# Gates between two layers: normalisation moved to ACT in blocks, products without a reader on PE, and an early table load

## The reference

```python
mask = top-20 channels of the context, per batch and position   # 0 or 1, (B, 32, 512)
crucial, rest = mask * xn, (1 - mask) * xn                      # xn = layernorm(x)
def gate(f, factor):
    z = conv1d(concat([max over channels of f, mean over channels of f * factor]), w)   # 7 taps, one output channel
    mu = mean(z); var = mean((z - mu) ** 2)                     # over all 64 * 512 values
    return sigmoid(relu((z - mu) * rsqrt(var + eps) * gamma + beta))
x = x + crucial * gate(crucial, 32 / 20) + rest * gate(rest, 32 / 12)
x = x + attention(layernorm(x)); x = x + layernorm(x) @ (W * block_mask).T
```

## Time and profile before

| | |
|---|---|
| median of three runs | 2092.75 us (2090.44 to 2094.00) |
| the profiled execution, its own time | 2093.99 us |
| its span | 2092.2 us |
| granted TensorE clock, mean | 0.987 of full |
| busy | PE 96%, DVE 62%, ACT 35%, POOL 33% |
| the gates' block, from layer 0's last reduction to layer 1's first DVE work | 1817.8 to 1835.4 us |

### The profile page before, as it was taken

How to read it: one execution, slowest core, us unless ns; L and a number is a source line. 1 busy time by engine, 2 the same in 40 slices (tenths; PEclk the granted TensorE clock), 3 DMA queues, 4 the chain that set the end, 5 groups by cost and what they waited for, 6 DMA issues and landing times. The chain is left out here.

```text
span 2092.2 us, 36562 instructions
## 1 busy us (share of the span) xinstructions
PE 2013.9 (96%) x11300; PEld 1564.8 (75%) x11300; DVE 1295.4 (62%) x4403; ACT 741.6 (35%) x2037; POOL 683.3 (33%) x1068
## 2 busy tenths in 40 slices
PE   7999999999999999999999999999899999779998
PEld 5878788887877888788787878887566666455664
DVE  3846548474564847547484664847477777667774
ACT  2434334343443434334343433433232323122232
POOL 4422324232332423323242332423332333133332
PEclk9999999999999999999999999999999999889999
DMA  7101001010010101001010010111100000000000
GB/s 295 32 15 34 22 24 30 24 30 24 24 30 14 40 14 31 23 24 30 24 30 24 24 30 14 31 46 41 46 1 1 1 0 30 1 1 21 21 15 26
DMA packets 51995, 62.19 MB, mean 30 GB/s; under 512 B 14193, under 2 KB 47665, under 8 KB 51042
## 3 DMA queue, kind: packets, MB, share of 16 engines
q1 hardware_dynamic: 51938, 61.46, 9.3%
HBM read 54.00 MB, written 4.29 MB: 28 GB/s over the span
## 5 line engine op out<-in xcount | busy, mean ns | idle before, releaser
L431 PE MATMUL psLane<-hid,WkT 128*128 128x289 f32 x1536 | 402.4, 407 | 0.0
L431 PEld LDWEIGHTS psLane<-hid,WkT 128*128 128x128 f32 x1536 | 283.3, 190 | 72.3
L644 ACT ACTIVATE probs<-psLane,nmax 128x289 f32<-128x289 f32 x256 | 126.2, 498 | 429.7 <-DVE nmax L751 429.7
L610 ACT ACTIVATE KT<-psLane 96x289 f32<-96x289 f32 (+2 forms) x384 | 155.8, 406 | 151.0 <-PE psLane L431 148.8
L353 POOL TENSOR_TENSOR w_o<-w_o 128x192 f32<-128x192 f32 x64 | 44.8, 700 | 460.6 <-ACT w_o L619 460.6
L789 DVE MAX8 top<-work 128x8 f32<-128x257 f32 x512 | 180.2, 414 | 2.7
L314 POOL TENSOR_TENSOR tails<-probs,unit 128x66 f32<-128x66 f32 x128 | 38.2, 299 | 431.0 <-ACT probs L644 400.2
L421 PE MATMUL psLane<-xnT,WqT 128*128 128x128 f32 x1536 | 176.6, 275 | 0.0
L421 PEld LDWEIGHTS psLane<-xnT,WqT 128*128 128x128 f32 x1536 | 174.7, 192 | 0.3 <-issue 0.3
L518 PE MATMUL psLane<-WoT,OT 128*128 128x512 f32 x384 | 169.2, 597 | 1.4 <-DVE OT L769 1.4
L774 DVE TENSOR_TENSOR X<-X,psLane 128x512 f32 (+1 forms) x16 | 11.0, 687 | 254.2 <-PE psLane L518 254.2
(11 more groups left out here) (211 smaller groups left out, 4129.6 us busy)
## 6 DMA issues: line engine op xcount, KB each, us to landing
hid<-in_ctxT SPq DMA_DIRECT2D x64, 514.0 KB, 3.8
y<-X SPq DMA_DIRECT2D x16, 256.0 KB, 2.0
X<-in_x SPq DMA_DIRECT2D x1, 3840.0 KB, 14.1
WqT<-in_WqT SPq DMA_DIRECT2D x4, 768.0 KB, 11.2
WoT<-in_WoT SPq DMA_DIRECT2D x1, 3072.0 KB, 20.9
Vtail<-Vlat SPq DMA_DIRECT2D x128, 24.0 KB
w_qkv<-in_w_qkv SPq DMA_DIRECT2D x2, 1536.0 KB, 6.3
w_ffn<-in_w_ffn SPq DMA_DIRECT2D x2, 1024.0 KB, 6.9
```

The source lines that it names most:

```text
L431: mm = pe.matmul(out[:, 0:S], WkT[:, c, P * k:P * k + P], hid[:, j, c, :], start=(c == 0), stop=(c == DC - 1))
L610: ins = act.activation(KT[at:at + hi - lo, j % 2, g, :], psKV[lo:hi, kv_bank(t, 7 * j + k), 0:S], ACT.Copy)
L644: act.activation(probs[:, g, :], psS[:, g % 2, 0:S], ACT.Exp, bias=nmax[:, g:g + 1], scale=XSCALE, accum_out=rsum[:, j % 2, g:g + 1]).then ...
```

## The change

`ones` is filled with -1/(B*D) instead of 1.0, so that a product with it gives minus a mean. A new helper `keep_busy` issues n products of `ones` with itself into a part of PSUM that nobody reads; 50 of them are added: 10 at the end of layer 0, 6 after the first sum, 12 after the second, and in layer 1, for tile 0 alone, 8 ahead of `turn_mix`, 10 ahead of `turn1` and 4 ahead of `qkv`. Each stands ahead of the wait of its stage.

In `mix_gates` the convolution's four column blocks lie in four banks with a semaphore step each. DVE multiplies a quarter of `w_ffn` by its mask, waits for a block and reduces it straight from PSUM; PE adds the four partial sums in one accumulated group. The squares are made by two activations from PSUM with minus the mean as bias and an accumulator. The power is one instruction of two columns. DVE makes a scale and an offset of two columns, and ACT applies relu with both from PSUM and then sigmoid, for the rest's part first, straight into `blend`, then for the crucial part; DVE is left with one subtraction. An activation of one column with Sigmoid stands at the head of the block, and one with Exp at the head of layer 1 on ACT.

```diff
@@ -899,7 +899,7 @@
         mix_gates(nc, neghalf, ps, Y, ones, blend, early["band"], affine, late, late_in)
-        layer1(nc, a, X, mask, ident, neghalf, x_tile, ps, bufs, blend, late)
+        layer1(nc, a, X, mask, ident, neghalf, x_tile, ps, bufs, blend, late, ones)
@@ -1077,7 +1077,7 @@
                 pool.wait_ge(zero_done, 5)
-                pool.memset(ones[:], 1.0).then_inc(ones_done, 1)
+                pool.memset(ones[:], -1.0 / (B * D)).then_inc(ones_done, 1)
                 pool.wait_ge(ones_done, 1 + 2 * TB)
@@ -1189,6 +1189,8 @@
                 "lora_up": lora_up, "turn3": lambda t, u: norm_turn(pe, n3, t, u, xn, high(u), ident)})
+            pe.wait_ge(ones_done, 1 + 2 * TB)
+            keep_busy(pe, ps[:, LANES - 1], ones, 10)
...
+def keep_busy(pe, out, ones, n):
+
+    for _ in range(n):
+        pe.matmul(out[:, 0:P], ones[:], ones[:], start=True, stop=True)
...
@@ -1360,88 +1368,95 @@
-        part = sb("part", [P, 2])
+        part = sb("part", [P, DC, 2])
+        squares = sb("squares", [P, 2])
+        minus_mean = sb("minus_mean", [P, 2])
-        step, mean_step = sem("mix_step"), sem("mean_step")
-        conv_done, sums_done, pow_done = sem("conv_done"), sem("sums_done"), sem("mix_pow_done")
-        sig_done = sem("sig_done")
-        conv = ps[:, 0, 0:DC * 2 * B]
-        sums = ps[:, 1, 0:2]
-        sums2 = ps[:, 2, 0:2]
...
+        conv = ps[:, 0:DC, 0:2 * B]
+        by_which = conv.rearrange("p c (w b) -> p w c b", w=2)
+        sums = ps[:, 0, 512:514]
+        sums2 = ps[:, 1, 512:514]
+        idle = ps[:, LANES - 1, 512:1024]
...
         def _(pe):
-            pe.wait_ge(mean_step, 2)
+            pe.wait_ge(means_done, 2)
             for o in range(DC):
                 pairs = [(i, ch) for i in (o - 1, o, o + 1) if 0 <= i < DC for ch in range(2)]
                 for n, (i, ch) in enumerate(pairs):
                     at = P * (o - i + 1)
-                    mm = pe.matmul(conv[:, 2 * B * o:2 * B * (o + 1)], band[:, ch, at:at + P],
+                    mm = pe.matmul(conv[:, o], band[:, ch, at:at + P],
                                    Y[:, i, ch].rearrange("p w b -> p (w b)"), start=(n == 0), stop=(n == len(pairs) - 1))
-            mm.then_inc(conv_done, 1)
-            pe.wait_ge(step, 2)
-            pe.matmul(sums, ones[:], part[:], start=True, stop=True).then_inc(sums_done, 1)
-            pe.wait_ge(step, 6)
-            pe.matmul(sums2, ones[:], part[:], start=True, stop=True).then_inc(sums_done, 1)
+                mm.then_inc(conv_done, 1)
+            pe.wait_ge(part_done, DC)
+            for o in range(DC):
+                mm = pe.matmul(sums, ones[:], part[:, o], start=(o == 0), stop=(o == DC - 1))
+            mm.then_inc(sums_done, 1)
+            keep_busy(pe, idle, ones, 6)
+            pe.wait_ge(squares_done, 2)
+            pe.matmul(sums2, ones[:], squares[:], start=True, stop=True).then_inc(sums_done, 1)
+            keep_busy(pe, idle, ones, 12)
 
         @block.gpsimd
         def _(pool):
-            pool.wait_ge(step, 7)
-            for w in range(2):
-                ins = pool.tensor_tensor(rstd[:, w:w + 1], moment[:, w:w + 1], neghalf[:], ALU.pow)
-            ins.then_inc(pow_done, 1)
+            pool.wait_ge(moment_ready, 1)
+            pool.tensor_tensor(rstd[:], moment[:], neghalf[:].to_broadcast([P, 2]), ALU.pow).then_inc(pow_done, 1)
 
         @block.scalar
         def _(act):
-            act.wait_ge(step, 9)
-            act.activation(Z[:].rearrange("p c w b -> p (c w b)"), Z[:].rearrange("p c w b -> p (c w b)"),
-                           ACT.Sigmoid).then_inc(sig_done, 1)
+            act.activation(scratch[:, 0:1], neghalf[:], ACT.Sigmoid).then_inc(scratch_done, 1)
+            act.wait_ge(mean_ready, 1)
+            for w in range(2):
+                act.activation(sq[:, :, w], by_which[:, w], ACT.Square, bias=minus_mean[:, w:w + 1],
+                               accum_out=squares[:, w:w + 1]).then_inc(squares_done, 1)
+            act.wait_ge(scale_done, 1)
+            act.wait_ge(offset_step, 2)
+            for k, w in enumerate((1, 0)):
+                act.activation(Z[:, :, w], by_which[:, w], ACT.Relu, bias=offset[:, w:w + 1], scale=scale[:, w:w + 1])\
+                    .then_inc(relu_done, 1)
+                act.wait_ge(relu_done, k + 1)
+                act.activation(blend[:, :, 0] if w else Z[:, :, 0], Z[:, :, w], ACT.Sigmoid).then_inc(sig_done, 1)
...
         @block.vector
         def _(dve):
...
             dve.wait_ge(late_in, 16 * LATE_LOADS)
-            dve.tensor_tensor(late["w_ffn"][:], late["w_ffn"][:], late["ffn_mask"][:], ALU.mult)
-            dve.wait_ge(conv_done, 1)
-            z = Z[:].rearrange("p c w b -> p (c w b)")
-            dve.tensor_copy(z, conv).then_inc(step, 1)
-            dve.wait_ge(step, 1)
-            dve.tensor_reduce(part[:], Z[:].rearrange(by_which), AX.XY, ALU.add).then_inc(step, 1)
+            for o in range(DC):
+                dve.tensor_tensor(late["w_ffn"][:, o], late["w_ffn"][:, o], late["ffn_mask"][:, o], ALU.mult)
+                dve.wait_ge(conv_done, o + 1)
+                dve.tensor_reduce(part[:, o], conv[:, o].rearrange("p (w b) -> p w b", w=2),
+                                  AX.X, ALU.add).then_inc(part_done, 1)
             dve.wait_ge(sums_done, 1)
-            dve.tensor_scalar(moment[:], sums, 1.0 / count, None, ALU.mult).then_inc(step, 1)
-            dve.wait_ge(step, 3)
-            dve.tensor_tensor(Z[:].rearrange("p c w b -> p c w b"), Z[:],
-                              moment[:].unsqueeze(1).unsqueeze(3).to_broadcast([P, DC, 2, B]), ALU.subtract)\
-                .then_inc(step, 1)
-            dve.wait_ge(step, 4)
-            dve.tensor_tensor(sq[:], Z[:], Z[:], ALU.mult).then_inc(step, 1)
-            dve.wait_ge(step, 5)
-            dve.tensor_reduce(part[:], sq[:].rearrange(by_which), AX.XY, ALU.add).then_inc(step, 1)
+            dve.tensor_scalar(minus_mean[:], sums, 1.0, None, ALU.mult).then_inc(mean_ready, 1)
             dve.wait_ge(sums_done, 2)
-            dve.tensor_scalar(moment[:], sums2, 1.0 / count, EPS, ALU.mult, ALU.add).then_inc(step, 1)
+            dve.tensor_scalar(moment[:], sums2, -1.0, EPS, ALU.mult, ALU.add).then_inc(moment_ready, 1)
             dve.wait_ge(pow_done, 1)
-            dve.tensor_tensor(Z[:], Z[:], rstd[:].unsqueeze(1).unsqueeze(3).to_broadcast([P, DC, 2, B]), ALU.mult)\
-                .then_inc(mean_step, 1)
-            dve.wait_ge(mean_step, 3)
-            dve.tensor_scalar(z, z, affine[:, 0:1], affine[:, 1:2], ALU.mult, ALU.add).then_inc(step, 1)
-            dve.wait_ge(step, 8)
-            dve.tensor_scalar(z, z, 0.0, None, ALU.max).then_inc(step, 1)
-            dve.wait_ge(sig_done, 1)
-            dve.tensor_copy(blend[:, :, 0, :], Z[:, :, 1, :])
-            dve.tensor_tensor(blend[:, :, 1, :], Z[:, :, 0, :], Z[:, :, 1, :], ALU.subtract)
+            dve.tensor_scalar(scale[:], rstd[:], affine[:, 0:1], None, ALU.mult).then_inc(scale_done, 1)
+            dve.wait_ge(scale_done, 1)
+            dve.tensor_tensor(offset[:], minus_mean[:], scale[:], ALU.mult).then_inc(offset_step, 1)
+            dve.wait_ge(offset_step, 1)
+            dve.tensor_scalar(offset[:], offset[:], affine[:, 1:2], None, ALU.add).then_inc(offset_step, 1)
+            dve.wait_ge(sig_done, 2)
+            dve.tensor_tensor(blend[:, :, 1, :], Z[:, :, 0, :], blend[:, :, 0, :], ALU.subtract)
...
+def layer1(nc, a, X, mask, ident, neghalf, x_tile, ps, bufs, blend, late, ones):
...
+        scratch = sb("scratch1", [P, 1])
...
+            def busy_until_first(t, n):
+
+                if isinstance(t, int) and t == 0:
+                    keep_busy(pe, high(LANES - 1), ones, n)
+
             def turn_mix(t, u):
+                busy_until_first(t, 8)
                 pe.wait_ge(s["mixed"], t + 1)
...
+            def turn1(t, u):
+                busy_until_first(t, 10)
+                norm_turn(pe, n4, t, u, xn, high(u), ident)
+
             def qkv(t, u):
+                busy_until_first(t, 4)
                 pe.wait_ge(n4["xnT"], t + 1)
...
             over_lanes(pe, SLOTS1, STARTS1, {
-                "turn_mix": turn_mix, "turn1": lambda t, u: norm_turn(pe, n4, t, u, xn, high(u), ident), "qkv": qkv,
+                "turn_mix": turn_mix, "turn1": turn1, "qkv": qkv,
...
+            act.activation(scratch[:], neghalf[:], ACT.Exp).then_inc(s["table_loaded"], 1)
             over_lanes(act, SLOTS1, STARTS1, {"xnT1": evac_xnT(n4), "evac_qk": evac_qk, "exps": exps, "spread_p": spread_p,
```

More of the change, by code:

```diff
@@ L1362, in mix_gates @@
         sq = sb("sq", [P, DC, 2, B])
-        part = sb("part", [P, 2])
+        part = sb("part", [P, DC, 2])
+        squares = sb("squares", [P, 2])
+        minus_mean = sb("minus_mean", [P, 2])
         moment = sb("moment", [P, 2])
         rstd = sb("mix_rstd", [P, 2])
-        step, mean_step = sem("mix_step"), sem("mean_step")
```

(45 more changed lines are left out.)

## The result

The changed kernel takes 2087.10 us (median of 8 runs, 2085.75 to 2089.41), the kernel before 2093.54 us beside it (8 runs, 2090.44 to 2095.88). The ratio is 0.9970, with a 95% interval of 0.9961 to 0.9979: 6.3 us faster, between 4.4 and 8.2. The profiled execution took 2086.80 us (span 2085.0, clock 0.995), against 2093.99.

A forecast was written before the change was run, and what follows sets the result against it. PE is busy 96% of the span; a serial chain of 17.6 us between the layers leaves it idle or slow. Gates 4.6 plus opening 1.8, less 1.7 for one slow-clock stay, is 4.7 off 2092.75: 2088.05 us, range 2085.3 to 2091.5.

The forecast's parts named there:

- rival A: The clock stays up everywhere behind 1818: 6.4 us won, 2086.3 us; chance 0.27.
- The gates' sum: Gates' block between the layers, PE at 1.00: layer 1 starts at 1830.8 instead of 1835.41, 4.6 us won.
- Moving it to ACT wins nothing: Gates' part behind the power, moved to ACT: lasts 3.4 us, as before.
- The opening's sum: Layer 1's opening at 1.00: Q, K and V begin at 8.75 as before and are 1.8 us shorter.
- The feared stay near 1835 to 1839: Around layer 1's start: one dip of the clock expected there, otherwise 1.00 for most of 1823 to 1850.
- idle products on the chain of waits: Sign that the forecast is wrong; the sum itself had 0.5 us lost to the ten before the first normalised tile.
- the table: Exponential table load of 1.28 us, moved to layer 1's head: already hidden, worth 0 (bounds 0 to 0.3).
- the tail's ten products: Layer 0's tail: they run under DVE's reductions, 1813.3 to 1817.8 at 0.50, 0.1 us at most past DVE.
- I take one: One stay at clock 0.50 on PE's path, costing 1.7 us, so 6.4 - 1.7 = 4.7 us won.
- C: Transposes do not hold the clock in layer 1's opening: 2.1 us won, 2090.65 us; chance 0.14.
- E: Clock at 0.50 from convolution to Q and K, twelve products outlast ACT: 9.3 us lost, 2102.0 us; chance 0.04.
- D: Idle products get in the way or ACT's chain is dearer: 2.9 to 3.8 us won, about 2089.5; chance 0.13.

The follow-up runs named there:

- e14: The changed kernel, unaltered, run again beside others: 2088.05 us, ratio 0.9964 to the kernel before.
- e12: The kernel before, unaltered, run once for a second profile: 2095.55 us profiled, no ratio.
- e6: The changed kernel without the early exponential activation at layer 1's head, run once: 2088.18 us profiled, no ratio.
- e1: The changed kernel without any of the 50 idle products and without the early exponential table: 2090.02 us, ratio 0.9984 to the kernel before.
- e10: The changed kernel with 12 more products at the head of layer 0's PE stream: 2086.31 us, ratio 0.9966 to the kernel before.
- e11: The change with 12 products at layer 0's head, 16 ahead of its last transposes, 6 instead of 10 ahead of `turn1`: 2087.33 us, ratio 0.9963 to before.
- e4: The changed kernel with each idle product turned into a transpose of the same size: 2090.64 us, ratio 0.9990 to the kernel before.
- e2: The kernel before with the 50 idle products put into the old gates and same places: 2090.53 us, ratio 0.9986 to the kernel before.
- e7: The changed kernel with 16 more products ahead of layer 0's last `turn3`: 2087.81 us, ratio 0.9976 to the kernel before.
- e13: The change with scale, offset and maximum on DVE and only the sigmoids on ACT, run once: 2087.95 us profiled, no ratio.
- e3: The changed kernel without the 8, 10 and 4 products at layer 1's opening: 2088.15 us, ratio 0.9970 to the kernel before.
- e5: The changed kernel without the 10 products at layer 0's tail: 2090.63 us, ratio 0.9989 to the kernel before.

## Why the prediction was right, and where it was off

It gave 2088.05 us in 2085.3 to 2091.5, and 4.7 us won; 2087.10 and 6.3 were measured, inside the range. Its 4.7 lies in the measured 4.4 to 8.2, near the lower end. The best estimate is the size of rival A (6.4), but not A's mechanism. That the total came out inside the range is in part luck: up to tile 1's Q and K the change's two profiles win 4.6 and 6.2 us (a and b, against the first profile of before), and c, which the sum held at nothing, wins 3.0 and 1.3 more.

**The gates' sum held.** The timeline of e14, where the convolution ran at 1.00, shows the case that was summed:

```profile
1821.38 4.73 PE L1398 MATMUL psLane<-Y,band 128*128 128x128 f32 x40 [1.24 <-DVE Y L1435]
...
1826.15 0.29 DVE L1441 TENSOR_REDUCE part<-psLane 128x2 f32<-128x128 f32 x1
...
1827.78 0.47 ACT L1420 ACTIVATE sq<-psLane,minus_mean 128x256 f32<-128x256 f32 x1 [5.50 <-DVE minus_mean L1444]
...
1828.60 0.20 ACT L1420 ACTIVATION_READ_ACCUMULATOR sq<-psLane,minus_mean 128x1 f32 x1
...
1829.51 0.70 POOL L1413 TENSOR_TENSOR mix_rstd<-moment,neghalf 128x2 f32<-128x2 f32 x1 [10.32 <-DVE moment L1446]
...
1830.70 0.23 DVE L1452 TENSOR_SCALAR mix_offset<-mix_offset,affine 128x2 f32<-128x2 f32 x1
1831.03 0.56 ACT L1425 ACTIVATE Z<-psLane,mix_offset,mix_scale 128x256 f32<-128x256 f32 x1 [2.23 <-DVE mix_offset L1452]
...
1833.70 0.69 DVE L1640 TENSOR_TENSOR lanes<-mask,blend 128x512 f32<-128x512 uint8 x1 [0.30 <-PEq L1362]
```

| step | predicted, us | e14, us |
|---|---|---|
| convolution's start to the last reduction's end | 5.06 | 5.06 |
| four sums and minus the mean | 1.35 | 1.34 |
| two squares | 1.05 | 1.02 |
| second sum and moment | 0.65 | 0.71 |
| power, two columns | 0.60 | 0.74 |
| three tiny DVE steps | 0.65 | 0.78 |
| relu, sigmoid, twice | 2.05 | 1.92 |
| subtraction and exit | 0.70 | 0.75 |
| convolution's start to layer 1 | 12.11 | 12.32 |

The power was sized from a one-column row of 0.55; with two columns it is 0.70. "Moving it to ACT wins nothing" held too: 3.49 us from the power's end to layer 1, against 3.39 in e12.

**The opening's sum held**: 1.8 predicted, 17.26 - 15.43 = 1.83 measured, and 15.43 (to 0.01) in all six other profiles that have the new gates and layer 1's products as the change has them. The eight products are free (they end at 1835.09, `turn_mix` starts at 1835.27). The ten hold `turn1` back: it starts 7.61 us after layer 1's start instead of 6.97, 0.64 where 0.5 was predicted, and the faster transposes give most of it back. The feared stay near 1835 to 1839 came in no profile of the change. One of the forecast's own signs of being wrong, idle products on the chain of waits, did come, at the price that the sum had given them.

**Terms taken as free that held**: the table (e6), the extra table loads (one load of 1.28 us in the gates serves Square, Relu and Sigmoid), the tail's ten products (they end at 1817.17, DVE's last reduction at 1818.23).

**The step that was mis-sized** is "I take one": one stay at 0.50 on PE's path, -1.7 us. Between the tail's end and layer 1's Q and K, the change's profiles show one stay in the convolution (worth 14.51 - 12.87 = 1.64, the price was right) or none (e14, e6). That alone puts the forecast 0 to 1.7 too low. The second part was not in the sum at all: it held the rest of layer 1 at no change, where 1.3 to 3.0 us were won. The ledger says by what: c is 234.0 to 234.3 with one stay after 1880 us, 235.6 to 235.8 with two, 237.0 to 237.1 with three, and so in fourteen profiles of fourteen. Both profiles of before have three, at the same places of the program; those of the change have one and two. A stay costs 1.5 us there. e1, with the clock as low at the start of layer 1 as before, has one, and e10 and e11, with the opening at 1.00, have three. So it isn't the opening's clock that decides. What sorts the profiles is where in the program the clock falls. In all five with three stays (before, e12, e4, e10, e11) they start 36.2 to 36.3, 217.1 to 217.2 and 224.0 us after tile 1's Q and K. In the five with two (e14, e2, e6, e7, e13) they start after 35.3 to 35.6 and 223.0 to 223.4 us, and in three of the four with one (the change, e1, e3) after 220.9 to 221.6, in e5 after 36.1. Kernels as different as before and e10 share their places, and two executions of the change don't, so c's gain can't be put down to the edit. What sets the places is open, and so is how much of c the change wins in a typical run: no run was made that sets them.

**A reading of the rows that was off.** The nine transposes of 1571.38 to 1572.53 start ahead of the stretch from 1571.5, so they fill 1.03 us of it and products 1.16, not 1.15 and 1.04. The rows thus spoke less clearly against C than the forecast says; e4 settles it.

**The rivals.** C fell by e4. E (twelve products that outlast ACT at a low clock) never came: in every profile with the change's gates and these products the clock was 1.00 when they began. D's dearer ACT chain was 0.13 cheaper than forecast. A described e14's and e6's profiles up to tile 1, but not that of the change, in which the clock fell once behind 1818.

## What to carry to other kernels

Where a serial stretch leaves the matrix engine idle and its clock falls, as it did here, the work behind takes up to twice the time: price it from rows at both levels, then ask if work without a reader, placed ahead of the wait, covers the rest without outlasting it. Here the shorter chain alone won 3.3 us and such filler alone 2.9, and of the filler the ten products in the last gap before the chain mattered most. Look for gains and losses of the clock over the whole span, not only where the edit is: here the count of short stays some 50 to 240 us after layer 1's start moved a profile by up to 3.0 us, more than the opening did (1.8). Count them before a difference of a few us between two profiles is put down to an edit.

## What the runs showed of the hardware that was not expected

- Filler is counted in instructions and must cover a time. Ten products take 4.02 us across a rise of the clock (the change), 4.31 in e14, 2.40 at 1.00 (e7, e11): filling one gap halves the cover of the next.
- A float32 transpose is one record: ten take 2.23 us at 0.50, and they raise the clock as products do (e4).
- A rest of 3.56 us ahead of the same convolution was followed by a stay in e11 and by none in e7, with the same kernel code there.
- A stay of 3.4 us cost 1.64 us in the convolution (the change against e14) and 1.3 to 1.7 in layer 1 (column c of the ledger), and profiles of quite different kernels have their late stays at the same distances behind tile 1's Q and K, within 0.1 us (before, e12, e4, e10, e11).
